# Value products of attention moved behind the next scores in parts of two batches, with separate places for the weights and VectorE's list steps between a tile's copies

## The reference

```python
scores = jnp.einsum('bhqd,bhkd->bhqk', q, k) * scale
scores = jnp.where(banned[None, None], -jnp.inf, scores)
probs = jax.nn.softmax(scores, axis=-1)
out = jnp.einsum('bhqk,bhkd->bhqd', probs, v)
```

## Time and profile before

| | |
|---|---|
| median of 3 runs | 787.65 us |
| the profiled execution, its own time | 789.38 us |
| its span in the trace | 787.3 us |
| mean granted TensorE clock | 0.983 |
| TensorE busy | 735.5 us (93%), 5167 matmuls |
| VectorE busy | 587.4 us (75%) |
| ScalarE busy | 473.1 us (60%) |
| GpSimd busy | 331.2 us (42%) |

### The profile page before, as it was taken

The page is one execution under the profiler, slowest core; times in us unless marked ns, Lnnn a source line. Parts: engine busy times, 40 slices in busy tenths (PEclk is TensorE's granted clock), DMA queues, the critical chain, the costliest instruction groups (busy, mean ns, idle before and its releaser), DMA issues.

```text
span 787.3 us, 14189 instructions
## 1 busy us (share of the span) xinstructions
PE 735.5 (93%) x5167; PEld 512.7 (65%) x5184; DVE 587.4 (75%) x1099; ACT 473.1 (60%) x1028; POOL 331.2 (42%) x329
## 2 busy tenths in 40 slices
PE   5988999999999999999987989999998999999993
PEld 4866777777777776777764777888874444444441
DVE  6986866886667866766665548878888999999882
ACT  4565666766676665766666314444455787667761
POOL 2011205213242134254553544445546677777661
PEclk9998999999999999999999999999999999999997
DMA  9300012214130322314311356555430233333231
GB/s 314 115 1 27 28 40 95 92 44 151 40 107 29 108 85 77 108 31 153 129 40 55 54 198 258 182 197 201 140 126 25 54 88 87 94 95 102 73 92 42
DMA packets 55474, 78.33 MB, mean 99 GB/s; under 512 B 36335, under 2 KB 38383, under 8 KB 53680
## 3 DMA queue, kind: packets, MB, share of 16 engines
q1 hardware_dynamic: 46336, 51.99, 20.6%
q0 software_dynamic: 8784, 24.93, 9.8%
q10 hardware_dynamic: 288, 0.52, 0.2%
HBM read 56.92 MB, written 17.59 MB: 95 GB/s over the span
## 4 chain that ended last, share of the span: by engine, by line
PE 62%; DVE 20%; issue 8%; ACT 5%; POOL 2%; DMA 1%; another core or an unknown queue 0%; ACTq 0%; SPq 0%; POOLq 0%; DVEq 0%
PE side_ps L889 17%; PE pT_ps L976 10%; PE e_z_ps L1528 7%; PE y_ps L1528 7%; PE pv_ps L998 5%; PE s_ps L948 5%; DVE h L1784 4%; ACT hq L1739 2%; DVE neg_max L724 2%; DVE hw_max L1800 2%; DVE hq_big L1831 2%; PE s_ps L956 2%; PE pT_ps L889 1%; DVE probs L745 1%; ACT f_gate L1746 1%
## 5 line engine op out<-in xcount | busy, mean ns | idle before, releaser
L548 ACT ACTIVATE probs<-s_ps,neg_max 128x512 f32<-128x512 f32 (+2 forms) x256 | 152.5, 611 | 17.9 <-DVE neg_max L724 16.4
L724 DVE TENSOR_REDUCE neg_max<-s_ps 128x2 f32<-128x1024 f32 (+2 forms) x128 | 124.6, 1015 | 36.1 <-PE s_ps L956 35.0
L976 PE MATMUL pT_ps<-ident,probs 128*128 128x128 f32 x832 | 116.5, 282 | 7.8 <-DVE probs L745 7.0
L560 ACT ACTIVATE probs<-pT_ps 128x512 f32<-128x512 f32 x96 | 57.5, 599 | 98.7 <-PE pT_ps L976 97.3
L976 PEld LDWEIGHTS pT_ps<-ident,probs 128*128 128x128 f32 x832 | 95.1, 145 | 23.0 <-DVE probs L745 9.7
L745 DVE COPY probs<-pT_ps 128x512 f32<-128x512 f32 x112 | 76.8, 685 | 39.1 <-PE pT_ps L976 36.2
L1695 POOL TENSOR_TENSOR xg_own<-h,ln_w_sb 128x512 f32<-128x512 f32 x63 | 81.9, 1308 | 37.9 <-DVE h L1784 37.8
L889 PE MATMUL side_ps<-w_hi 128*128 128x512 f32 x172 | 71.0, 413 | 0.0
L412 POOL TENSOR_TENSOR aT_hi<-norm,one_col 128x512 fp32r<-128x512 f32 x15 | 15.6, 1041 | 126.6 <-DVE norm L736 88.4
L889 PE MATMUL side_ps<-w_hi,w_lo 128*128 128x512 f32 x172 | 67.5, 392 | 0.0
L889 PE MATMUL side_ps<-w_lo,w_hi 128*128 128x512 f32 x172 | 67.0, 390 | 0.0
(11 more groups left out here) (290 smaller groups left out, 1779.4 us busy)
## 6 DMA issues: line engine op xcount, KB each, us to landing
w_piece<-w_ffn SPq DMA_DIRECT2D x24, 512.0 KB
w_stage<-w_ffn SPq DMA_DIRECT2D x12, 1024.0 KB
xres<-x POOLq DMA_DIRECT2D x4, 1024.0 KB, 6.4
xn<-x SPq DMA_DIRECT2D x3, 1024.0 KB
x<-xres POOLq DMA_DIRECT2D x3, 1024.0 KB, 4.8
xn<-c SPq DMA_DIRECT2D x2, 1024.0 KB, 5.1
v_next<-c SPq DMA_DIRECT2D x2, 1024.0 KB, 7.5
xn<-x SPq DMA_DIRECT2D x4, 256.0 KB, 3.4
```

Source lines behind the costliest of these rows:

```text
L548: nc.scalar.activation(weights[qt][:, h, at:at + width(qt)], s_ps[:, h, 0:width(qt)], ACT.Exp, bias=neg_max[:, qt % 2, h:h + 1], accum_out ...
L560: nc.scalar.activation(out, turned_p, ACT.Identity).then_inc(slot_copied[0], 1)
L724: nc.vector.tensor_reduce(neg_max[:, qt % 2, 2 * s:2 * s + 2], s_ps[:, 2 * s:2 * s + 2, 0:width(qt)], AX.X, ALU.max, negate=True).then_inc ...
L976: last = nc.tensor.transpose(pT_ps[:, k % 2, h * P:h * P + P], weights[qt][:, h, a:z], ident[:])
```

## The change

`values_late` names pairs whose value products TensorE does one unit later: behind the next unit's scores and its transposes of slots 0 and 1. They are, in the last batch, both pairs of groups 1 and 2 and the first pair of group 3; in batch 0, the second pair of group 0 and both pairs of group 1. Where the second pair is late, VectorE's multiply `attn_of` moves behind its copy of slot 1. The second pair's weights get a place of their own (6.2 KB more of each partition). In batch 0 the list steps of units (0,3), (1,2) and (1,3) and the normalisations of units (0,3) and (1,0) move between VectorE's copies of slots 1 and 3; those that stood behind unit (0,3) are now in units (1,0) and (1,1).

```diff
-        probs = sb("probs", [P, 2 * GH * SEQ + GH * BAND])
+        probs = sb("probs", [P, 2 * GH * (SEQ + BAND)])
...
+        def values_late(b, g, pair):
+
+            return (b == BATCH - 1 and 1 <= g < HG and (g, pair) != (HG - 1, 2)) or b == 0 and (g, pair) in ((0, 2), (1, 0), (1, 2))
...
-                2: probs[:, 2 * GH * (SEQ - BAND // 2):].rearrange("p (u h n) -> p u h n", u=2, h=GH)}
+                2: probs[:, 2 * GH * SEQ:].rearrange("p (u h n) -> p u h n", u=2, h=GH)}
...
-                if qt == 0 and 0 < g < HG:
+                follows_late = qt == 0 and 0 < g < HG and values_late(b, g - 1, 2)
+                if qt == 0 and 0 < g < HG and not follows_late:
                     attn_of(b, g - 1)
...
                 copy_slot(b, g, qt, 1)
+                if follows_late:
+                    attn_of(b, g - 1)
+                if (b, g) == (0, 1):
+                    (slots_addressed, experts_of_tiles, rows_given, rows_addressed)[qt]()
+                    assert done[0] == ROUTE_STEPS if qt == 1 else done[0] == ROUTE_DENSE if qt == 3 else True
+                if (b, g, qt) == (0, 0, TT - 1):
+                    for t in (0, 1):
+                        normalize(1, t)
+                if (b, g, qt) == (0, 1, 0):
+                    for t in (2, 3):
+                        normalize(1, t)
...
-                if prepare and qt == TT - 1:
+                if g and prepare and qt == TT - 1:
                     for t in (0, 1):
                         normalize(coming, t)
-                if not last and (g, qt) == (1, 0):
+                if b and not last and (g, qt) == (1, 0):
                     for t in (2, 3):
                         normalize(b + 1, t)
...
-            for qt, route_parts in enumerate(((tiles_needed, rows_started), (slots_given,), (), (slots_addressed, experts_of_tiles))):
+            for qt, route_parts in enumerate(((tiles_needed, rows_started), (slots_given,), (), ())):
...
-                        if (b, g, qt) == (0, 1, 2):
-                            rows_given()
-                        if (b, g, qt) == (0, 1, 3):
-                            rows_addressed()
-                            assert done[0] == ROUTE_DENSE
...
                 transpose_slot(b, g, qt, 1)
+                if qt == 2 and values_late(b, g, 0):
+                    attend_pair(b, g, 0)
+                if qt == 0 and g and values_late(b, g - 1, 2):
+                    attend_pair(b, g - 1, 2)
...
-                if qt % 2:
+                if qt % 2 and not values_late(b, g, qt - 1):
                     attend_pair(b, g, qt - 1)
```

More of the change, by code:

```diff
@@ L857, in vector_program @@
                     part()
-            assert done[0] == ROUTE_STEPS
             def batch(b, last):
```

## The result

The changed kernel took 789.71 us in the median of 18 runs (787.87 to 791.81), the kernel before 786.69 us in the median of 18 (785.43 to 789.62): a ratio of 1.0029 with a 95% interval of [1.0018, 1.0039], which is 2.3 us **slower**. The forecast was 785.6 us and a gain of 2.0; the result is outside its range and on the other side.

A forecast was written before the change was run, and what follows sets the result against it. TensorE, 93% busy, was taken as the bound, with idle time and half clock only in thin units without projection. Last batch +2.4 and batch 0 -0.4 gave 2.0 us off the 787.65 median: 785.6 us, range 782.7 to 788.4.

The forecast's parts named there:

- The last batch: Groups 1 to 3 of the last batch: late products fill thin units, a gain of 2.4 us in sum.
- The units (2,0) to (3,1): Last batch, unit by unit: gains 1.55 in (2,1), 2.15 in (2,3), 1.5 in (3,1); loss 1.2 in (2,2).
- hand-overs: TensorE's switches between kinds of work: products to transposes taken as 0.33 us, 0.5 us in a unit taking products in.
- (2,2) staying near 4.0 (the path was never TensorE's): Sign of being wrong: the last batch's unit (2,2) would not lengthen from 4.02 to about 5.25 us.
- rival A: The clock too: no half-clock stretch remains in either place, gain about 4.1 us, 783.5 us; chance 0.2.
- The pair (1,2) of batch 0: Its products leave the wait before X0 and are paid in the full unit (2,0): loss 1.6 us.
- rival C: Slower: half clock falls on filled units (2,2), (3,0), (3,2) and batch 0's (2,0), 1.6 us each, 788.9 to 792.0; chance 0.07.
- The sentence on the page's rule: On the rule that idle gaps throttle TensorE: the trace was said to agree because full units stay at clock 1.00.
- the +0.9 forecast for the list steps out of the way in (1,2) and (1,3): Batch 0: four VectorE list steps move from before the maxima into idle time, gain 0.9 us up to X0.
- Batch 0 up to (1,2): Gains 1.1 and 2.65 us by (1,1)'s end, less 2.4 for products returning in (1,2): 0.25 us left.
- What is gained passes on whole: Behind attention the first expert gather waits for the stored x1, so attention's gain was to reach the end undiminished.
- Rivals B and D: B: the wait only moves, 787.3 us, chance 0.2. D: the order doesn't change, 787.65 us, chance 0.02.

The follow-up runs named there:

- e2: Changed kernel with late products in the last batch alone, VectorE's steps in their old places: 784.28 us, ratio 0.9962 to the kernel before.
- e1: The kernel before again, with no edit, as a second profile: 788.53 us, ratio 1.0014.
- e9: Changed kernel plus 12 unused identity transposes filling TensorE's idle time before X0 in batch 0's unit (1,3): 787.58 us, ratio 1.0002 to the kernel before.
- e8: Changed kernel with only the pair (0,2) late in batch 0: 786.69 us, ratio 0.9984 to the kernel before.
- e10: e4 plus six long-satisfied waits in VectorE's stream (1328 instructions): 785.38 us, ratio 0.9975 to the kernel before.
- e12: The kernel of e6 measured again: 783.51 us, ratio 0.9949 to the kernel before.
- e6: Changed kernel without batch 0's pair (1,2) late and with VectorE's steps in their old places: 783.46 us, ratio 0.9952 to the kernel before.
- e11: Changed kernel with only (0,2) late in batch 0 and VectorE's steps in their old places: 782.66 us, ratio 0.9937 to the kernel before.
- e3: Changed kernel without the last batch's late products, so batch 0's part alone with VectorE's moved steps: 793.59 us, ratio 1.0079 to the kernel before.
- e4: Changed kernel with only batch 0's pair (1,2) put back: 786.31 us, ratio 0.9981 to the kernel before.
- e5: Kernel before plus three long-satisfied waits in VectorE's stream, two instructions more (1325): 789.37 us, ratio 1.0021 to the kernel before.
- e7: Changed kernel with nothing late in batch 0, the last batch late and VectorE's steps moved: 786.17 us, ratio 0.9987 to the kernel before.

## Why the prediction was wrong

**The last batch: right in mechanism, too small.** Every unit went the way that was worked out, and most by more. Entering group 2 (0.8 forecast), 402.50 - 396.08 = 6.42 us became 404.52 - 398.95 = 5.57: 0.85. The units (2,0) to (3,1) were forecast at 5.8, 5.0, 5.25, 5.3, 5.85 and 5.0 us and took 5.71, 4.53, 4.28, 5.12, 5.32 and 4.53. The term mis-sized most is TensorE's time in a unit that takes products in, of which the 0.5 us of hand-overs is the largest part. TensorE in the timeline of the kernel after, unit (2,2):

```profile
416.53 1.93 PE L1008 MATMUL pv_ps<-probs,v_sb 128*32 128x256 f32 x32
418.39 0.28 PE L982 MATMUL pT_ps<-ident,sinks 128*16 128x128 f32 x1
```

The next transposes begin at 418.39, before the last product has ended at 418.46: products to transposes costs nothing, where the forecast took 0.33 from the row of products to projection. (2,2) had its products for 0.26 us more than its 4.02 instead of 1.2. Of the 1.0 us between the forecast's terms and the 4.28 the hand-overs are 0.5. TensorE's own work took 2.42 (414.76 to 416.53 and 418.39 to 419.04) instead of 2.77, and the products 1.86 instead of 2.02. One sign of being wrong was "(2,2) staying near 4.0 (the path was never TensorE's)"; it stayed near, but TensorE is busy 4.28 of 4.28 us, so it is the bound there as forecast. In (2,1) and (3,1), 4.53 instead of 5.0, the half clock went that the earlier trace rows shows in (2,1) at 0.74: this much of rival A came true. The price behind them was nearly right: from the scores of (3,2) to the experts' first gather it was 23.74 us against 21.44, 2.3 lost where the forecast had 2.4. The gather starts at 457.75 against 460.11, inside the 1 to 4 us that were forecast. From the scores of (1,1), 383.53 before and 386.19 after, to that gather the two traces differ by 5.0 us. That is more than the 3.0 that e2 shows by its runs, whose interval of 2.0 to 4.0 takes in the forecast of 2.4; so that the sum was too small rests on the traces. They overstate it, in part since the profile of before held more half clock than most of its executions (e1's takes 0.75 us less there).

**The pair (1,2) of batch 0: the failing step.** The text had it: "With the products gone the cover goes: TensorE stands idle there about as long as they took, X0 starts at about 87, and TensorE pays 1.2 + 0.4 for the products in the full unit (2,0). Loss 1.6." X0 started at 87.25, after 2.11 us idle. But the products cost 2.04, not 1.6, and the idle time brought the half clock onto the full unit behind it, 1.40 more (e9), a term that the sum put at nothing. The forecast priced this only as rival C, at 1.6 a unit, a chance of 0.07, and named (2,0) of batch 0 among its places. (C's price is itself not the sum of its terms: 1.07 and as much again are 2.1, not 1.6.) In the profile of the kernel after one of these four places fell to half clock; the three in the last batch did not (1.00 in (2,2) and (3,0) in the rows above), and instead batch 0's (1,2), which C did not name, did: 0.85. In other traces with the same last batch (3,0) fell too: 6.33 to 6.54 us at 0.74 to 0.78 in e8, e9, e10 and e12, against 5.31 to 5.33 at 1.00 in the other six. The argument against C was "the full units after thin ones today stand at 1.00", and the forecast's own rows spoke against it: the last batch's (2,1) is full, 6.56 of 6.56, at 0.74, and batch 0's (1,1) nearly so, 6.62 of 6.91, at 0.75. The sentence on the page's rule, "The trace agrees in that the full units stay at 1.00", fails by the same two rows. What stands ahead of these two are the longest idle times of TensorE in the units before them, in the kernel before:

```profile
66.94 0.65 PE L976 MATMUL pT_ps<-ident,probs 128*128 128x128 f32 x4 [1.88 <-DVE probs L745]
...
407.74 0.66 PE L976 MATMUL pT_ps<-ident,probs 128*128 128x128 f32 x4 [1.75 <-DVE probs L745]
```

In the kernel after such rows stand ahead of (1,2), 2.16 us, and of (2,0), 2.11 us, the two full units at 0.85 and 0.84:

```profile
68.23 1.09 PE L986 MATMUL pT_ps<-ident,probs 128*128 128x128 f32 x8 [2.16 <-DVE probs L749]
```

It is no rule: in batch 0 of the kernel after 2.18 us stand ahead of (1,0), and in its last batch 1.61 ahead of (3,0), and both units stay at 1.00. It can even differ between two executions of one program. In e6 and e12, the same kernel, 1.61 us of idle time stand ahead of (3,0) in both, and the unit reads

```profile
420.87:426.20 5.33, 5.05 (x58) 3.33 (x59) 4.21 (x6) 4.04 (x12) 0.42 (x1) 1.00 0.01 3
```

```profile
419.49:426.02 6.53, 6.53 (x58) 4.33 (x58) 4.02 (x5) 4.20 (x12) 0.07 (x1) 0.74 0.01 3
```

But it was the reading to make: idle times of 1.75 and 1.88 us stood ahead of half clock in the rows of before, and the forecast itself made one of that length ahead of a full unit. There the half clock belongs in the likeliest sum, at some share of its price, and not in a rival of 0.07. And the +0.9 forecast for the list steps out of the way in (1,2) and (1,3) was had: (1,3) went from 8.94 to 8.09, but the pair's loss stands against it.

**Batch 0 up to (1,2): gained, and then paid back with more.** Forecast +0.25. Counted from the scores of (0,3), the kernel after reaches the scores of (1,2) 2.44 us earlier than before and those of (1,3) 0.73 later: -0.73, where +0.25 was forecast. The products in (1,2) cost 8.23 - 5.06 = 3.2, not 2.4, since that unit too fell to 0.85; at 1.00, in e6, they cost 2.1. VectorE in (1,0), in the timeline of the kernel after:

```profile
63.31 0.69 DVE L740 TENSOR_TENSOR norm<-pv_ps,norm 128x512 f32<-128x512 f32 x1
63.92 0.17 DVE L834 CAST slot<-slot_f 128x16 int32<-128x16 f32 x1
64.12 1.03 DVE L835 TENSOR_SCALAR slot_tile<-slot 128x16 int32<-128x16 int32 x1
65.19 0.18 DVE L836 TENSOR_SCALAR slot_row<-slot 128x16 int32<-128x16 int32 x1
65.40 1.15 DVE L837 SCALAR_TENSOR_TENSOR slot_at<-slot_row,slot_tile 128x16 int32<-128x16 int32 x1
66.58 1.00 DVE L627 TENSOR_SCALAR xn<-xn,bn_mv,rstd 128x512 f32<-128x512 f32 x2
67.50 0.68 DVE L749 COPY probs<-pT_ps 128x512 f32<-128x512 f32 x1
68.10 1.83 DVE L728 TENSOR_REDUCE neg_max<-s_ps 128x2 f32<-128x776 f32 x2
```

The maxima start at 68.10, forecast 68.3. But by another sum: the multiply was early and the four list steps took 2.53 us instead of 0.8, two of them 1.03 and 1.15 us while GpSimd splits the attention beside them.

**"What is gained passes on whole": wrong by 1.5 us.** From the experts' first gather to the first gate above it is 130.37 us before and 130.20 after, so attention's times do pass on to the feed-forward block, but there two more instructions in VectorE's stream cost 1.45 us. The forecast counted what the moved steps cost where they stand, and did not ask what a change in the stream's length does to a stage that nothing in the change touches.

**Rivals B and D** did not come: no wait took the place of the removed one in the last batch, and the order did change.

## What to carry to other kernels

Work that stands on the path under a wait may be its cover: taken out, the engine idles there, the work is paid in full where it goes, and on TensorE the idle time can put the unit behind it at half clock (2.04 + 1.40 us here for 1.29 us of products and those of the sinks), so move work only out of places where the freed time is used. A change of several like parts should be timed part by part: here one of the eight late pairs cost 3.8 us where the five of the last batch gained 3.0, and a version without it, without (1,0) and without the moved VectorE steps was 0.6% faster than the kernel before. When two traces are compared, follow the difference of like instructions through the whole program: a step in it where the code is unchanged (1.45 us here) is a cost of its own with a cause of its own.

## What the runs showed of the hardware

In this case the number of VectorE's instructions ahead of a place went together with whether 0.24 us of idle time stands there with no releaser: 1323 in the whole stream (before, e1, e2, e6, e11, e12) no, 1325 (after, e3, e4, e5, e7, e8, e9) yes, 1328 (e10) no. Why it falls at this place was not settled; that it comes and goes with instructions that only lengthen the stream is shown by e5 and e10, once each.

Two engines' order at one moment can hold a short instruction for a long one: the quantising instruction takes 0.48 us, and 1.96 when a GpSimd weighting gets in first. The Trainium skill, SBUF — State Buffer, section "SBUF: two separate sides", says that GpSimd and a VectorE instruction of certain kinds (one in a 2-port mode, or with two inputs in SBUF) share a port pair as an exclusive lock, and that whichever starts first holds it for its whole instruction. Whether the quantising is of these kinds no run here shows. The trace agrees in that the quantising ends at 597.95, 0.3 behind GpSimd's end. But it had stood since 595.99, ahead of the third weighting's start at 596.4, so here a waiting VectorE instruction was passed by a GpSimd one that started later. The integer list steps of 16 elements, 0.17 to 1.03 and 1.15 us, look like the same: the two long ones start at 64.12 and 65.40, beside GpSimd's two splits of 1.04 us at 64.08 and 1.31 us at 65.20. That was not tried by itself.

The busy share of a unit does not tell its own clock: (0,3) of the kernel after is busy 2.92 of 5.70 us at 1.00, and (2,0) is busy throughout at 0.84. Nor do the idle times ahead of it tell it for sure: behind 1.6 to 2.2 us of idle time the next unit stood at half clock for a part in some traces and at 1.00 in others, in two executions of one kernel too (e6 and e12).
